# Cross-attention block in float32 on one core: query projection per team of batches instead of per batch, value bias added to the values, keys stored by dimension

## The reference

```python
q = x @ Wq + bq          # 100 x 512
k = c @ Wk + bk          # 361 x 128
v = c @ Wv + bv          # 361 x 128
attn = softmax(q_head @ k_head.T / 4 + mask)     # per head, 100 x 361
out = (attn @ v_head, all heads) @ Wo + bo       # 100 x 512
x1 = layernorm(out + x) * gamma + beta
```

## Time and profile before

| what | value |
| --- | --- |
| median of 3 runs | 677.18 us (675.15 to 677.86) |
| the profiled execution's own time | 673.3 us |
| its span, first to last instruction | 671.5 us |
| busy share of the span | PE 96%, DVE 74%, ACT 59%, POOL 59% |
| share of 16 DMA engines' time | 66.9% |
| DMA packets | 61072, 109.67 MB; 11621 of them under 512 B |

### The profile page before, as it was taken

How to read it: one execution, slowest core, us unless ns; L and a number is a source line. 1 busy time by engine, 2 the same in 40 slices (tenths; PEclk the granted TensorE clock), 3 DMA queues, 4 the chain that set the end, 5 groups by cost and what they waited for, 6 DMA issues and landing times.

```text
span 671.5 us, 11880 instructions
## 1 busy us (share of the span) xinstructions
PE 646.0 (96%) x3737; PEld 470.4 (70%) x3737; DVE 497.7 (74%) x1455; ACT 394.8 (59%) x588; POOL 398.4 (59%) x255
## 2 busy tenths in 40 slices
PE   5998999999999999999999999999999999989987
PEld 2455666777777878777777768787777777756455
DVE  1547787887687787878787878878787888786742
ACT  3232675766657666656766676766567656656421
POOL 4328676775475766667665657676676667554220
PEclk9999898999999999999999999999999999999999
DMA  8898767576785776868584778666786857644212
GB/s 265 266 176 182 182 148 157 124 143 163 141 271 100 244 138 198 162 193 177 130 235 108 230 107 256 123 208 154 198 171 162 193 126 158 116 87 137 89 46 72
DMA packets 61072, 109.67 MB, mean 163 GB/s; under 512 B 11621, under 2 KB 49573, under 8 KB 60498
## 3 DMA queue, kind: packets, MB, share of 16 engines
q1 hardware_dynamic: 61010, 108.91, 66.9%
HBM read 86.37 MB, written 22.10 MB: 162 GB/s over the span
## 4 chain that ended last, share of the span: by engine, by line
PE 71%; DMA 9%; POOL 6%; issue 5%; DVE 3%; SPq 3%; ACT 1%; POOLq 0%; DVEq 0%; ACTq 0%
PE mx_ps L581 11%; PE work L540 10%; PE work L541 9%; PE work L542 9%; PE o_ps L597 7%; PE work L654 5%; PE work L705 5%; POOL pr L2490 4%; DMA late<-r_dr 4%; PE sc_ps L568 3%; PE sc_ps L569 3%; PE sc_ps L561 3%; PE work L610 2%; DMA k_dr<-k_l 1%; PE work L728 1%
## 5 line engine op out<-in xcount | busy, mean ns | idle before, releaser
L1549 DVE CUSTOM_DVE_ANT_0 mx_ps<-mx_ps,mask_n 100x361 f32<-100x361 f32 x512 | 270.9, 543 | 64.9 <-PE mx_ps L581 60.0
L2490 POOL TENSOR_TENSOR pr<-pr,mask_t 128x800 f32<-128x800 f32 x124 | 236.1, 1912 | 65.4 <-ACT pr L2056 65.2
L581 PE MATMUL mx_ps<-ks,qs 96*100 96x362 f32 x512 | 182.0, 372 | 3.9 <-DMA qs<-q_dr 1.9
L2063 ACT ACTIVATE pr<-pr 128x1200 f32<-128x1200 f32 x128 | 149.4, 1206 | 13.1 <-POOL pr L2490 6.1
L2056 ACT ACTIVATE pr<-sc_ps 128x800 f32<-128x800 f32 x124 | 104.0, 838 | 73.4 <-PE o_ps L597 47.2
L581 PEld LDWEIGHTS mx_ps<-ks,qs 96*100 96x100 f32 x512 | 84.7, 167 | 42.4 <-DVE mx L1549 11.9
L1535 DVE TENSOR_TENSOR pr<-sc_ps,mask_t 128x400 f32<-128x400 f32 x124 | 70.8, 571 | 24.1 <-PE sc_ps L561 15.3
L2502 POOL TENSOR_TENSOR c_l<-cT,c_h 128x1448 fp32r<-128x1448 f32 x16 | 55.0, 3439 | 52.5 <-ACT c_h L2090 52.5
L1549 DVE DVE_READ_ACCUMULATOR2_ANT mx<- 100x1 f32 x512 | 72.0, 141 | 0.0
L597 PE MATMUL o_ps<-pr,va 128*32 128x400 f32 (+1 forms) x768 | 71.2, 503 | 0.2 <-ACT pr L2063 0.2
L654 PEld LDWEIGHTS work<-late 128*128 128x128 f32 (+1 forms) x384 | 49.6, 191 | 6.9 <-issue 5.9
(11 more groups left out here) (167 smaller groups left out, 1232.4 us busy)
## 6 DMA issues: line engine op xcount, KB each, us to landing
qs<-q_dr SPq DMA_DIRECT2D x128, 100.0 KB, 4.3
late<-in_ctx SPq DMA_DIRECT2D x16, 768.0 KB, 6.6
cT<-in_ctxT SPq DMA_DIRECT2D x16, 724.0 KB, 4.9
ks<-k_dr SPq DMA_DIRECT2D x128, 90.5 KB, 4.0
late<-in_ctxT SPq DMA_DIRECT2D x16, 724.0 KB, 5.8
o_dr<-o_s SPq DMA_DIRECT2D x30, 200.0 KB, 3.3
xT<-in_xT SPq DMA_DIRECT2D x16, 200.0 KB, 4.2
q_dr<-q_h SPq DMA_DIRECT2D x16, 200.0 KB, 4.9
```

The source lines that it names most:

```text
L581: nc.tensor.matmul(mx_ps[0:L, n % 2, 0:SP2], qs[p][0:TERMS, g, L * j:L * (j + 1)], ks[p][0:TERMS, g, 0:SP2], start=True, stop=True).then_i ...
L1549: V.tensor_tensor_reduce(out=src, in0=src, in1=mask_n[p][:, :], scale=1.0, scalar=-3.0e38, op0=ALU.add, op1=ALU.max, accum_out=mx[p][:, n: ...
L2063: A.activation(t, t, ACT.Exp).then_inc(ex_ok, 1)
L2490: G.tensor_tensor(t, t, mask_t[p][:, 1:3, :].unsqueeze(2).to_broadcast([P, 2, J, L]), ALU.add).then_inc(sc_pool, 1)
```

## The change

The 16 batches are put in six teams, of 2, 2, 3, 3, 3 and 3. The queries of a team are projected together and turned at once: the stationary operand is a 128 x 128 block of `Wq`, the moving one the team's rows of `x` (200 or 300 columns), for each of four column blocks j, in 4 steps of three matmuls. The natural form, its bias step and the four transposes per batch go; the bias is one column per block, added in `q_high` and `q_low`; the factor 1/4 is in the split weights. `queries_out(t, j)` writes one block for a whole team, in pieces of 400 B, as soon as it is there. The value bias is added in `v_cols` and `bias_row` goes. Keys are written by dimension and padded to 384, so that a row of a key stack is one piece of 6144 B. Every engine's list is written anew, with nothing else added or removed per batch; in it the first context is loaded later, the second `x` earlier. One buffer instead of two holds the turned maxima.

```diff
+TEAMS = ((0, 2), (2, 2), (4, 3), (7, 3), (10, 3), (13, 3))
...
-        x_h, x_l = sb("x_h", [P, JL], F32R), sb("x_l", [P, JL], F32R)
+        x_h, x_l = sb("x_h", [P, KT * TB * L], F32R), sb("x_l", [P, KT * TB * L], F32R)
...
-        k_dr = nc.dram_tensor("k_dr", (2, 2, P, SP2), F32, kind="Internal").ap()
-        q_dr = nc.dram_tensor("q_dr", (2, 2, P, JL), F32, kind="Internal").ap()
+        k_dr = nc.dram_tensor("k_dr", (2, 2, HD, KVH, SC * P), F32, kind="Internal").ap()
+        q_dr = nc.dram_tensor("q_dr", (B, 2, P, J, L), F32, kind="Internal").ap()
...
             def stacks_in(b, half, r0, r1):
                 p = b % 2
                 if r0 == 0:
-                    wait(sp, q_out, 32 * (b + 1))
+                    wait(sp, q_out, 32 * J * (team(b) + 1))
...
-                    sp.dma_start(ks[p][HD * r:HD * (r + 1), gs, 0:SP2].bitcast(F32),
-                                 k_dr[p, r // 2, :, :].rearrange("(g d) s -> d g s", d=HD)[:, gs, :]
+                    sp.dma_start(ks[p][HD * r:HD * (r + 1), gs, :].bitcast(F32), k_dr[p, r // 2, :, gs, :]
                                  ).then_inc(st_in[half][p], 16)
...
+            def queries_out(t, j):
+                b0, n = TEAMS[t]
+                wait(sp, qh_ok, J * t + j + 1)
+                wait(sp, ql_ok, J * t + j + 1)
+                for r, src in ((0, q_h), (1, q_l)):
+                    sp.dma_start(q_dr[b0:b0 + n, r, :, j, :].rearrange("b p l -> p b l"),
+                                 src[:, 0:n * L].bitcast(F32).rearrange("p (b l) -> p b l", l=L)).then_inc(q_out, 16)
...
-                sp.dma_start(k_dr[p, 0, :, :], k_h[:, :].bitcast(F32)).then_inc(k_out, 16)
+                sp.dma_start(k_dr[p, 0, :, :, :].rearrange("d g s -> g d s"), k_h[:, :].bitcast(F32)).then_inc(k_out, 16)
...
+            def q_part(t, j, k0, k1):
+                b0, n = TEAMS[t]
+                js = slice(P * j, P * (j + 1))
...
                 if k0 == 0:
-                    bank(1, q_nat, b + 1)
+                    bank(1, ql_ok, J * t + j + 1)
                 for k in range(k0, k1):
-                    mm = product(work[0:L, 1, :], x_h[:, xs], x_l[:, xs], wq_h[:, k, :], wq_l[:, k, :], k, KT - 1)
+                    mm = product(work[:, 1, 0:n * L], wq_h[:, k, js], wq_l[:, k, js], xs_h[:, k, 0:n, :],
+                                 xs_l[:, k, 0:n, :], k, KT - 1)
...
-            def bias_row(j0, j1):
...
-            def turn_q(b):
...
-            def q_natural(b):
...
+            def q_low(t, j):
+                V.scalar_tensor_tensor(q_l[:, 0:n], work[:, 1, 0:n], bq_c[:, j:j + 1], q_h[:, 0:n].bitcast(F32),
+                                       ALU.add, ALU.subtract).then_inc(ql_ok, 1)
...
-                A.activation(vT[:, :], work[:, 1, 0:SP2], ACT.Copy).then_inc(vT_ok, 1)
+                A.activation(vT[:, :], work[:, 1, 0:SP2], ACT.Identity, bias=bv_c[:, 0:1]).then_inc(vT_ok, 1)
...
-                A.activation(q_h[:, :], work[:, 1, 0:JL], ACT.Copy, scale=0.25).then_inc(qh_ok, 1)
+                A.activation(q_h[:, 0:n], work[:, 1, 0:n], ACT.Identity, bias=bq_c[:, j:j + 1]).then_inc(qh_ok, 1)
```

The start of SP's new list, and a middle stretch:

```diff
+            x_turned_in(0)
             weights_q()
             fold_m_in(0)
+            x_turned_in(1)
+            weights_o()
             biases()
+            fold_m_in(1)
+            fold_m_in(2)
+            queries_out(0, 0)
+            weights_k()
             ctx_turned_in(0)
...
+            maxima_in(8, 0)
+            keys_out(9)
+            mask_in(9)
+            rows_out(7, 0)
+            mask_turned_in(9)
+            result_out(5)
+            stacks_in(9, 0, 0, 2)
+            stacks_in(9, 0, 2, 4)
```

More of the change, by code:

```diff
@@ L40, in alone, with team @@
     return b == END and g >= 4
+def team(b):
+    return next(t for t, (b0, n) in enumerate(TEAMS) if b0 <= b < b0 + n)
 def ring(b, par, dmas=1):
@@ L602, in turn_maxima @@
                 p = b % 2
+                if b == 0 and half == 0:
+                    pe.wait_ge(zero_ok, 2)
                 pe.wait_ge(a_mx, NH * b + 16 * (half + 1))
@@ new lines, in _ @@
+            y_sum(3)
+            y_stats(3)
+            maxima(5, 22, 23)
+            y_moments(3)
+            centre(3)
+            q_low(3, 2)
+            shift(3)
+            maxima(5, 23, 24)
+            add_mask(5, 0)
+            maxima(5, 24, 25)
+            x1_low(3)
+            maxima(5, 25, 28)
+            add_mask(5, 1)
+            maxima(5, 28, 32)
+            add_mask(5, 2)
+            maxima(6, 0, 3)
+            maxima_low(5, 1)
+            maxima(6, 3, 4)
+            add_mask(5, 3)
@@ new lines, in _ @@
+            maxima(7, 6, 7)
+            reciprocals(5)
+            maxima(7, 7, 9)
+            add_mask(6, 4)
+            maxima(7, 9, 13)
+            cx_low(4)
+            maxima(7, 13, 14)
+            row_sum(4)
+            maxima(7, 14, 17)
+            q_low(4, 0)
+            add_mask(6, 5)
+            residual(4)
+            maxima(7, 17, 18)
+            maxima_low(7, 0)
+            add_mask(6, 6)
+            maxima(7, 18, 19)
+            k_low(8)
+            add_mask(6, 7)
@@ new lines, in _ @@
+            add_mask(7, 7)
+            maxima(8, 20, 24)
+            y_sum(6)
+            y_stats(6)
+            y_moments(6)
+            centre(6)
+            q_low(4, 2)
+            shift(6)
+            maxima(8, 24, 25)
+            add_mask(8, 0)
+            maxima(8, 25, 26)
+            x1_low(6)
+            maxima(8, 26, 30)
+            add_mask(8, 1)
+            maxima(8, 30, 32)
+            add_mask(8, 2)
+            maxima(9, 0, 3)
+            maxima_low(8, 1)
+            add_mask(8, 3)
@@ new lines, in _ @@
+            maxima(9, 3, 6)
+            row_max(6)
+            reciprocals(7)
+            maxima(9, 6, 10)
+            add_mask(8, 4)
+            maxima(9, 10, 12)
+            cx_low(6)
+            maxima(9, 12, 13)
+            row_sum(6)
+            q_low(4, 3)
+            add_mask(8, 5)
+            maxima(9, 13, 16)
+            residual(6)
+            maxima(9, 16, 18)
+            maxima_low(9, 0)
+            maxima(9, 18, 19)
+            k_low(10)
+            add_mask(8, 6)
@@ new lines, in _ @@
+            add_mask(10, 6)
+            residual(8)
+            maxima(11, 16, 18)
+            maxima_low(11, 0)
+            maxima(11, 18, 20)
+            k_low(12)
+            add_mask(10, 7)
+            maxima(11, 20, 22)
+            y_sum(9)
+            y_stats(9)
+            y_moments(9)
+            q_low(5, 2)
+            centre(9)
+            shift(9)
+            maxima(11, 22, 24)
+            add_mask(11, 0)
+            x1_low(9)
+            maxima(11, 24, 25)
+            add_mask(11, 1)
@@ L2066, in output @@
                 act.wait_ge(pv_mm[half], b + 1)
-                if b == 0 and half == 0:
-                    act.wait_ge(bo_mm, 1)
                 if b == END and half == 1:
```

3274 lines of the change are left out of this document (2334 added, 940 removed).

## The result

The changed kernel takes 685.5 us (median of 20 runs), the kernel before 675.6 us beside it; the ratio is 1.0138, with a 95% interval of 1.0117 to 1.016. It is slower by 1.4 per cent where 665.5 us and a gain were forecast. The profiled execution took 686.7 us, its span 684.9 (before 673.3 and 671.5).

What follows compares the result with a forecast made beforehand. PE was taken to bound the kernel from 120 us on. The terms +3.0 - 2.0 - 14.2 + 1.5 = -11.7 us took the median of 677.2 to 665.5 us, range 656 to 669, chance 0.62.

Steps and rivals of the forecast that it cites:

- the paragraph on DMA pieces: Query and key transfers change piece sizes; 2.2 us of slack before the stack's reader, so 0 in the sum.
- the stacks come late: Key write and first-half stack loads land later; PE waits 1.8 us in 13 batches, 23 us: 689 us; chance 0.07.
- Steps 4 and 5: Start: later context delays first head product, +3.0 us; then less PE and DVE work up to batch 2's heads, -2.0.
- Step 4: Start: first context queued behind more loads, first head product +3.0 us later; bounds 0 and +5.
- times at full speed hold: Whole kernel: clock is full in all but a few early slices, so no clock term in the sum.
- the forecast's prices: PE query work: 3.10 us per batch before; after, 0.145 us per 300-column and 0.109 per 200-column product.
- Step 1: Query projection on PE: 38.3 instead of 49.6 us over 16 batches, saving 11.3; 0.145 us per 300-column product.
- narrow blocks: PE's query products cost 0.17 us each, sum -7.2 us, time 670 us; chance 0.10.
- Step 6: PE behind the start of batch 2's heads: query work 26.1 instead of 40.3 us, -14.2 us.
- second rival: Steady part: PE's saving turns into waits on bank 1, DVE or ACT; half lost, 672.6 us; chance 0.15.
- Steps 2 and 3: Bias row gone, 4.3 us of PE at the start; DVE saves 0.5 us a batch; neither counted separately in the sum.

Runs made afterwards that it cites:

- keys-alone run: Kernel before with only the keys written and read by dimension: 683.0 us, ratio 1.0115.
- filler runs: Eight extra 512-column products ahead of the first scores: in the changed kernel 684.0 us, 1.0172; in that with loads reordered, keys and queries permuted, 670.0 us, 0.9935.
- old keys: Changed kernel with its keys written and read as in the kernel before: 678.1 us, ratio 1.0028.
- mended kernels: Changed kernel, first loads reordered, key weights' columns permuted: 672.9 us, 0.998; also with wide, wrongly placed query writes 673.0, 0.9987; or query columns permuted 671.4, 0.9942.

## Why the prediction was wrong

**The step that failed first is the paragraph on DMA pieces**, with its zero in the sum. It had the right rule and the right rival (*the stacks come late*: key write, first-half stack loads, PE waits), and put 0.07 on it because one batch showed 2.2 us of slack. The Trainium skill (DMA: Bandwidth & Descriptors, Why a DMA increments its semaphore by 16 and not by 1) let the key write use eight engines instead of sixteen. The runs agree in direction: 4.41 us by groups against 2.06 for the same bytes over 128 rows. How many engines a write used is not in the rows.

The failure was the slack, twice over. First, it used the median landing of one load, 4.3 us, where all eight must have landed. The very load of the earlier trace rows took 6.4 us, from its issue at 311.48 to about 317.9, and its reader starts at 317.99: 0.1 us of slack, and not 2.2.

```profile
L239 SPq DMA_DIRECT2D qs<-q_dr x1: 426/426/426, 311.5 to 311.5; - x1
...
DMA to landing us min/median/max: 6.4/6.4/6.4
```

In the keys-alone run batch 9's heads waited until 358.64, 6.7 us behind the last issue at 351.90. Second, it read one batch: 6.5 us lie there between the last load's issue and its reader, and in batches 10 to 13 of the same trace 5.2 to 5.5. So several batches had next to no slack, and 1.0 us of later key write cost 7.8 us in the kernel before and 7.4 in the changed one, 0.5 us a batch. The rival's price, 23 us for data 4.0 us late, took the first 2.2 of them as free; measured were 7.5 us for the first 1.0, so its threshold of 3.4 us was too high. Its signs, a wait of a us or more per batch and key writes landing after 6 us, did not come either.

**Steps 4 and 5 (start: +3.0 - 2.0)** were wrong by 12.9 us: +13.9 at batch 2's milestone. Step 4 had the later context, and its upper bound of +5, but two waits were missing. The bias load stands behind the output weights in the same list, with a DVE step behind it (2.3 us of PE). A block of the second team stands ahead of the first heads (2.95 us). And the sum has no term for the clock: *times at full speed hold* was read from the kernel before. These are the stretches from the start to batch 2's milestone, changed kernel first (columns as in the earlier trace rows):

```profile
0.00:130.02 130.02, 107.91 (x477) 71.34 (x478) 72.68 (x206) 55.08 (x79) 64.14 (x41) 0.88 0.74 175
```

```profile
0.00:116.15 116.15, 102.46 (x430) 62.92 (x431) 70.47 (x204) 52.02 (x71) 65.17 (x41) 0.96 0.80 195
```

PE stood idle 22.1 us where it had stood idle 13.7. To the lower clock it lost an estimated 0.12 x 130 = 16 us against 0.04 x 116 = 5, both from these rows. So 8 us more of idle time and some 11 us more at the lower clock, less about 5 us of work that is gone (4.3 of it the bias row), make the 13.9. This divides the time and names no cause: the clock fell behind standstills, and the filler runs above show that taking such a fall away need not move the end. Query work was also moved forward, but little: by the forecast's prices the ten blocks up to this milestone are 13.9 us and the four batches before 12.4. Reordering the loads gives about 2.7 us of the total back.

**Step 1 (product prices)** was right: 0.14 us per 300-column product, against the rival *narrow blocks* with 0.17. **Step 6** was right from batch 4 on, once the keys are out of the way. Behind batch 4's milestone lie ten of the old projections and eleven of the new blocks, by the forecast's prices 31.0 - 19.1 = 11.9 us, and with the old keys and in two of the three mended kernels of the table 11.3 to 11.7 us are won; in the third, in an execution 5.8 us above its median, 4.0. The changed kernel wins 5.6. Between batches 2 and 4, where the forecast had a further 2.3 us, the mended kernels lose 1.9 to 5.3. The *second rival* holds in small: of the 5.7 us in eight steady batches 1.4 to 2.0 are lost in three of the four kernels, while PEld waits 12 us in place of 4. That is about a third, and not half of the saving.

**Steps 2 and 3** (bias row, DVE): their zeros were right. The bias row alone is worth 0.9999, and DVE's 10 us less bring nothing.

**Put together:** the forecast gain was 11.7 us and the result a loss of 9.4. Of the 21 us between, 7.4 are the key write, shown by undoing it, and about 2.7 the first loads, whose undoing moved the time by hardly more than its uncertainty. Some 11 us remain, since the mended kernel stands at 0.994 to 0.998 and not 0.983. The table says where they are: by the forecast batch 4's milestone comes 1.3 us earlier than before, and in the three mended kernels it comes 6.3 to 11.9 us later; 1.4 to 2.0 us more are in the steady part. What causes them stays open. The new hand-written order is argued for by the old order's 5.2 us of waits at about the same saving, and was not tested by rewriting it; a part for the clock is not excluded.

Both kernels are beaten by the kernel before with permuted keys (0.9963) and by the changed one with loads reordered and keys and queries permuted (0.9942, with filler 0.9935). The last two can't be told apart from the first.

## What to carry to other kernels

When a change alters the shape of a transfer that a chain goes through, don't ask whether anybody waits for it now, but how late it may land: take the smallest slack over all periods, and the last landing of a group, not the median of one load. If a layout is wanted in another order, permute the weights' columns so that the producing tile is already in that order, and the write stays one plain run. And a saving on the busiest engine counts only where it is also what ends last: here from batch 4 on, not in the 190 us before.

## What was not expected of the hardware

- A 192-KB write of 128 rows of 1,536 bytes had landed 2.0 us after issue (median), the 181-KB write of 128 rows of 1,448 bytes 3.3 us, and the 192-KB write in eight groups released its waiter 4.4 us after issue against 2.1 for the plain one. Length of the rows and padding were not told apart.
- 16,384 write pieces of 400 bytes more or fewer made no difference to the time (1.0121 against 1.0138), while 17,000 more in a second set cost 17 us, 9 of them also with wide pieces.
- In the changed kernel a standstill of 2.6 us ahead of the first scores was followed by some 20 us at 1.2 GHz, and one of 1.6 us in the mended kernel by some 14. Standstills of 2.3 and 2.95 us earlier in the changed kernel, and one of 1.8 us at the same place in the kernel before, were followed by 3.6 us each. So the length of the standstill did not set that of the slow stretch. Eight filler products took the stretch away in one kernel and halved it in another, without a measurable change of the time.
